# Self-attention in straight code on all engines, and one on-chip sum done by an accumulating transfer instead of GpSimd

## The chip, the cores and the metric

One core of a Trainium2 chip runs the whole program. Its engines work side by side and meet at semaphores: TensorE (PE) multiplies, and loads its weights (PEld) beside that; VectorE (DVE) and ScalarE (ACT) compute and read the matmuls' results; GpSimd (POOL) computes and issues transfers; SyncE (SP) only issues transfers. 16 DMA engines move the data. The metric is the device time of one execution in microseconds (us), median of the runs of a kernel.

## What is computed

A transformer block on x (2 x 2048 tokens, 512 features): self-attention with 16 heads of 32, attention to a short context, and an MLP, each with a layer norm ahead and a residual behind it. The change is in the self-attention, so this is the part that matters (cut):

```python
xn = layer_norm(x, ln0_w, ln0_b)
qkv = xn @ qkv_w.T
q, k, v = jnp.split(qkv, 3, axis=-1)
q, k, v = (_heads(q), _heads(k), _heads(v))       # B, 16 heads, 2048, 32
attn = jnp.einsum('bhnd,bhmd->bhnm', q, k) * SCALE
attn = jax.nn.softmax(attn, axis=-1)
sa = _merge(jnp.einsum('bhnm,bhmd->bhnd', attn, v)) @ sa_proj_w.T
x = x + sa
...
```

Everything is float32. The softmax of one query runs over all 2,048 keys of its batch.

## The kernel before

The phases follow each other: `token_phase` (norm and q, k, v), `self_phase` (the attention itself, functions from L1253 on), a small context phase, cross attention, another `token_phase`, and the MLP. Only `self_phase` is changed.

**Tiling.** The 128 features of four heads are a group. A stage is 512 queries of one group; there are 2 batches x 4 groups x 4 = 32 stages. A stage runs over 2,048 keys in 16 tiles of 128 keys, for four heads: 64 pieces of scores [128 keys x 512 queries].

**Two passes.** The first pass computes the scores to find each query's maximum (64 matmuls into `first`, L1538; VectorE reduces each, L1707). The maxima are turned once per stage by a matmul against the identity (`turn_max`, L1560), split and put beside the queries as extra rows. The second pass (64 matmuls into `second`, L1568) computes the scores less the maximum; ScalarE takes the exponential into `expo` (L1657), which holds 8 tiles of keys. `weigh` (L1581) multiplies them by the values into `weighted`, 128 of the matmuls that the profile counts.

**The order on TensorE** is written out by hand. A stage has eight blocks. In a block, eight matmuls of the second pass of this stage alternate with eight of the first pass of a later one; behind them come those of `weigh` for the two tiles of the block before. Behind block 1 stands `add_up` for the stage before: the sums of its exponentials.

**The sums of the exponentials** are the denominators, one per head and query. GpSimd adds the exponentials of two neighbouring tiles of keys, all four heads at once: `add_pair` (L1474 to L1478), eight pairs a stage, 128 x 2048 elements. A pair's tiles can be overwritten by ScalarE when it is summed. The pair sums go to four parts of the buffer `part_sum`. Pairs 0 and 1 make h0 and h1, and pairs 2 to 5 are added to these in turn by a transfer that accumulates in place: `add_half` (L1480 to L1484), issued by GpSimd when the pair's sum is done; pairs 2 and 4 go from part p0 to h0, pairs 3 and 5 from p1 to h1. Its landing is told by the semaphores `half_added[0]` and `half_added[1]`, 16 each time. Pair 6 is summed to p0 and added to h1 by GpSimd itself (L1514, the merge). Pair 7 is summed to p1. In the next stage the parts change roles: the new h0 is the old p0 and the new p0 the old h0, while h1 and p1 stay.

`add_up` (L1585) then lets ones-matmuls sum over the keys of a part, in three sets: h0, h1 (with pair 6 in it) and p1 (pair 7). The total is copied by ScalarE (L1674), spread by SyncE, inverted by VectorE (L1724), spread again, and GpSimd multiplies the stage's result by it (`divide`, L1489).

**What sets the order around the change.** Each engine runs its own list in order; an instruction that waits holds all behind it on its engine. GpSimd's list per stage is: pairs 0, 1, 2, transfer, pair 3, transfer, `divide` of the stage before, pair 4, transfer, pair 5, transfer, pair 6, merge, pair 7. `pair_done` counts nine per stage (`n_adds`).

**Loops.** TensorE, ScalarE and SyncE have stage 0 written out, then a loop of 3 rounds of 8 stages, then 7 stages written out. VectorE's loop repeats every stage (29 times), GpSimd's every two stages (15 times). In loops a semaphore's target is computed with register instructions. Before a DMA, a wait against a register stands alone with an increment of its own (`wait_alone`); a wait against a number stands by itself.

## Time and profile before

| | |
|---|---|
| median of 3 runs | 3608.2 us (3604.48 to 3614.65) |
| the profiled execution | 3612.71 us, of which the span in the profile is 3610.9 us |
| mean TensorE clock granted in it | 0.939 of full speed |
| self-attention, first to last matmul of its kind | some 323 to 2049 us of the span |

| engine | busy in the span | share |
|---|---|---|
| PE | 3297.7 us | 91% |
| PEld | 2149.8 us | 60% |
| DVE | 2085.2 us | 58% |
| POOL | 1743.7 us | 48% |
| ACT | 1544.2 us | 43% |

Times in rows are in microseconds from the span's start. A row of a timeline has the start, the duration, the engine, the line of the code, the operation, what it writes and reads with shapes, how many instructions were put together, and in brackets the idle time of the engine just before, with what ended it. `issue` there means that the engine waited for nothing that the profile shows. `self_second` is the buffer `second`, in which the totals and the turned maxima have a place too. Matmuls overlap, so a matmul's duration is longer than the distance to the next one.

### The profile page before, as it was taken

What the parts mean: (1) busy time and instruction counts of PE and PEld (TensorE: products, weight loads), DVE (VectorE), ACT (ScalarE), POOL (GpSimd) and SP (SyncE); (2) the same over time, 40 slices, a digit from 0 to 9 for tenths busy, and PEclk for the clock granted to TensorE, in tenths of its full rate; (3) what the DMA queues carried; (4) which work ended last, traced back from release to release, by engine and by line L of the source; (5) the groups of instructions that cost most, each with busy time, mean ns of one, the idle gap of its engine ahead of it and who ended that gap; (6) DMA issues with size and microseconds to landing.
All of it is one profiled execution on the core that took longest, in us unless ns stands there. A gap on an engine that the chain in (4) does not pass through costs nothing. (4 is left out here: it accounts for less than half of the span.)

```text
span 3610.9 us, 52559 instructions
## 1 busy us (share of the span) xinstructions
PE 3297.7 (91%) x16448; PEld 2149.8 (60%) x16448; DVE 2085.2 (58%) x3635; ACT 1544.2 (43%) x2826; POOL 1743.7 (48%) x539
## 2 busy tenths in 40 slices
PE   7998999999999999999999668898968599999999
PEld 5885555555555555555555156566526488888887
DVE  4445877777877777787776025767646542222222
ACT  3230566666666566666666312444423221111111
POOL 0001798888898888889889622343332100000000
PEclk9997999999999999999999778999958799999999
DMA  4447358465664746566455343344325731111110
GB/s 171 180 163 194 78 108 168 103 141 113 127 135 101 165 99 143 114 126 136 99 121 106 89 141 105 122 118 126 93 98 198 263 113 47 47 47 46 47 47 24
DMA packets 195911, 420.97 MB, mean 117 GB/s; under 512 B 33602, under 2 KB 56712, under 8 KB 176240
## 3 DMA queue, kind: packets, MB, share of 16 engines
q1 hardware_dynamic: 173167, 282.80, 25.8%
q0 software_dynamic: 18432, 134.23, 19.1%
q8 instruction: 137, 2.24, 0.3%
q10 hardware_dynamic: 4096, 1.06, 0.1%
q14 instruction: 79, 0.64, 0.1%
HBM read 154.47 MB, written 102.82 MB: 71 GB/s over the span
## 5 line engine op out<-in xcount | busy, mean ns | idle before, releaser
L1707 DVE TENSOR_REDUCE self_part_max<-self_first 128x1 f32<-128x512 f32 x2048 | 1253.0, 679 | 372.5 <-PE self_first L1538 371.9
L1657 ACT ACTIVATE self_expo<-self_second 128x512 f32<-128x512 f32 x2048 | 1042.4, 625 | 504.2 <-PE self_second L1568 500.8
L1477 POOL TENSOR_TENSOR self_part_sum<-self_expo 128x2048 f32<-128x2048 f32 x256 | 1194.3, 4675 | 99.5 <-ACT self_expo L1657 59.9
L1538 PE MATMUL self_first<-self_k,self_q 96*128 96x512 f32 x2048 | 863.5, 429 | 26.4 <-DMA self_k<-k_t 12.8
L1568 PE MATMUL self_second<-self_q,self_k 98*128 98x512 f32 x2048 | 832.5, 408 | 14.7 <-DVE self_max_low L1719 9.8
L1538 PEld LDWEIGHTS self_first<-self_k,self_q 96*128 96x128 f32 x2048 | 401.8, 196 | 330.7 <-DVE self_part_max L1707 173.8
L1581 PE MATMUL self_weighted<-self_expo,self_v_sb 128*32 128x512 f32 x4096 | 498.1, 605 | 0.0
L1568 PEld LDWEIGHTS self_second<-self_q,self_k 98*128 98x128 f32 x2048 | 393.7, 193 | 161.5 <-ACT self_expo L1657 49.6
L2047 DVE CAST mlp_h_high<-mlp_h 128x512 fp32r<-128x512 f32 x128 | 54.8, 428 | 508.1 <-PE mlp_out_sum L61 507.0
L2022 ACT ACTIVATE mlp_h<-mlp_hidden_sum,mlp_b_col 128x512 f32<-128x512 f32 x128 | 88.1, 688 | 603.7 <-PE mlp_hidden_sum L61 603.6
L1581 PEld LDWEIGHTS self_weighted<-self_expo,self_v_sb 128*32 128x32 f32 x4096 | 107.6, 109 | 241.2 <-ACT self_expo L1657 134.3
L989 ACT ACTIVATE cross_expo<-cross_second 77x512 f32<-77x512 f32 x256 | 144.7, 591 | 217.6 <-PE cross_second L840 213.6
L738 POOL TENSOR_TENSOR cross_pair_sum<-cross_expo 77x2048 f32<-77x2048 f32 x32 | 146.2, 4567 | 182.0 <-ACT cross_expo L989 182.0
L59 PE MATMUL mlp_hidden_sum<-mlp_xt_high,mlp_w_high 128*128 128x512 f32 x512 | 203.8, 398 | 24.4 <-DMA mlp_xt_low<-xn_t 24.4
L60 PE MATMUL mlp_hidden_sum<-mlp_xt_low,mlp_w_high 128*128 128x512 f32 x512 | 203.2, 397 | 0.0
L60 PE MATMUL mlp_out_sum<-mlp_w_low,mlp_h_high 128*128 128x512 f32 x512 | 202.4, 395 | 0.0
L61 PE MATMUL mlp_hidden_sum<-mlp_xt_high,mlp_w_low 128*128 128x512 f32 x512 | 202.3, 395 | 0.0
L61 PE MATMUL mlp_out_sum<-mlp_w_high,mlp_h_low 128*128 128x512 f32 x512 | 202.2, 395 | 0.0
L59 PE MATMUL mlp_out_sum<-mlp_w_high,mlp_h_high 128*128 128x512 f32 x512 | 201.9, 394 | 0.0
L1514 POOL TENSOR_TENSOR self_part_sum<-self_part_sum 128x2048 f32<-128x2048 f32 x32 | 146.7, 4584 | 71.8 <-DMA self_part_sum<-self_part_sum 71.8
L1112 DVE TENSOR_REDUCE cross_row_max<-cross_first 128x2 f32<-128x308 f32 x256 | 113.6, 455 | 90.9 <-PE cross_first L823 90.9
L1482 POOL DMA_DIRECT2D self_part_sum<-self_part_sum x128 | 111.8, 873 | 74.9 <-POOL self_part_sum L1477 60.4
(163 smaller groups left out, 4019.3 us busy)
## 6 DMA issues: line engine op xcount, KB each, us to landing
self_part_sum<-self_part_sum POOLq DMA_DIRECT2D x128, 1024.0 KB, 7.5
self_k<-k_t SPq DMA_DIRECT2D x96, 256.0 KB, 10.3
self_q<-q_t SPq DMA_DIRECT2D x93, 256.0 KB, 8.1
cross_q<-cross_r_high SPq DMA_DIRECT2D x256, 64.0 KB, 2.0
qkv_x<-in_x SPq DMA_DIRECT2D x8, 1024.0 KB, 5.3
v<-qkv_v_sb SPq DMA_DIRECT2D x32, 256.0 KB, 2.0
q_t<-qkv_r_high SPq DMA_DIRECT2D x32, 256.0 KB, 2.0
q_t<-qkv_r_low SPq DMA_DIRECT2D x32, 256.0 KB, 2.3
```

The lines of the kernel that those rows point to most:

```text
L59: nc.tensor.matmul(out, left_high, right_high, start=first, stop=False)
L60: nc.tensor.matmul(out, left_high, right_low, start=False, stop=False)
L61: return nc.tensor.matmul(out, left_low, right_high, start=False, stop=last)
L738: nc.gpsimd.tensor_tensor(pair_sum[0:width, g % pair_slots], expo[0:width, u], expo[0:width, u + 1], ALU.add).then_inc(pair_done, 1)
L989: nc.scalar.activation(expo[0:width, unit % e_slots, a], second[0:width, at % s_ring], ACT.Exp, scale=scale).then_inc(exp_done, 1)
L1477: nc.gpsimd.tensor_tensor(to, expo[:, t % p_slots], expo[:, (t + 1) % p_slots], ALU.add).then_inc(pair_done, 1)
L1514: nc.gpsimd.tensor_tensor(part_sum[:, h1], part_sum[:, h1], part_sum[:, p0], ALU.add).then_inc(pair_done, 1)
L1538: nc.tensor.matmul(first[:, n % f_ring], q[0:base, c % q_slots, a, s * P:(s + 1) * P], k[0:base, c // stages_per_group % 2, a, k0:k0 + TOK ...
L1568: nc.tensor.matmul(second[:, s_slot[n]], k[0:exp_rows, c // stages_per_group % 2, a, t * P:(t + 1) * P], q[0:exp_rows, c % q_slots, a], st ...
L1581: mm = nc.tensor.matmul(weighted[cols], v_sb[:, t, cols], expo[:, t % p_slots, a], start=t == 0, stop=t == n_k - 1)
L1657: nc.scalar.activation(expo[:, t % p_slots, a], second[:, s_slot[n]], ACT.Exp, scale=scale).then_inc(exp_done, 1)
L1707: nc.vector.tensor_reduce(part_max[:, a * SUB + s, k:k + 1], first[:, n % f_ring], AX_X, ALU.max).then_inc(first_read, 1)
```

## The change

On every engine the loops of the self-attention become loops of the generator: all 32 stages are written out, and every wait is against a number. GpSimd's merge of pair 6 (L1514) is gone. Instead pair 6 is added to h0 by a fifth accumulating transfer, issued behind its sum, so `half_added[0]` counts 48 a stage, and `pair_done` counts eight. `add_up` takes the parts in another order, h1, then pair 7 (p1), then h0. Pair 0 of a stage waits for the landing of the fifth transfer of the stage before, since it writes to the part that this reads; pair 1 waits for the first set of ones-matmuls instead of the first two, and pair 2, which writes over the old h0, for all three.

```diff
-    n_adds = n_pairs + 1
...
-                with sp.Fori(0, rounds - 1) as r:
+                for r in range(rounds - 1):
...
                 def add_half(i, p, u, half, part):
-                    ge(pool, pair_done, n_adds * i + p + 1, alone=True)
+                    ge(pool, pair_done, n_pairs * i + p + 1, alone=True)
...
                 def add_pairs(i, c):
                     h0, h1, p0, p1 = sum_parts(c)
-                    ge(pool, pair_done, n_adds * i)
+                    ge(pool, half_added[0], 48 * i)
                     add_pair(i, 0, part_sum[:, h0])
-                    ge(pool, total_done, n_sums * (i - 1) + 2)
+                    ge(pool, total_done, n_sums * (i - 1) + 1)
                     add_pair(i, 1, part_sum[:, h1])
+                    ge(pool, total_done, n_sums * i)
                     add_pair(i, 2, part_sum[:, p0])
                     add_half(i, 2, 0, h0, p0)
-                    ge(pool, total_done, n_sums * i)
                     add_pair(i, 3, part_sum[:, p1])
...
                     add_pair(i, 6, part_sum[:, p0])
+                    add_half(i, 6, 0, h0, p0)
                     ge(pool, half_added[1], 32 * i + 32)
-                    ge(pool, pair_done, n_adds * i + 7)
-                    nc.gpsimd.tensor_tensor(part_sum[:, h1], part_sum[:, h1], part_sum[:, p0], ALU.add).then_inc(
-                        pair_done, 1)
                     add_pair(i, 7, part_sum[:, p1])
...
-                with pool.Fori(1, stages // 2) as r:
+                for r in range(1, stages // 2):
...
-                    for n, part in enumerate((h0, h1, p1)):
+                    for n, part in enumerate((h1, p1, h0)):
                         if n == 0:
-                            ge(pe, half_added[0], 32 * (i + 1))
+                            ge(pe, half_added[1], 32 * (i + 1))
                         elif n == 1:
-                            ge(pe, pair_done, n_adds * i + n_pairs)
+                            ge(pe, pair_done, n_pairs * (i + 1))
                         else:
-                            ge(pe, pair_done, n_adds * (i + 1))
+                            ge(pe, half_added[0], 48 * (i + 1))
...
-                with pe.Fori(0, rounds - 1) as r:
+                for r in range(rounds - 1):
...
-                with act.Fori(0, rounds - 1) as r:
+                for r in range(rounds - 1):
...
-                with dve.Fori(1, stages - 2) as i:
+                for i in range(1, stages - 2):
```

The semaphores of one phase are used again by the next, so the lists below name them by the first phase's names: `qkv_xt_high_done` is `exp_done`, `qkv_xt_ready` is `pair_done`, `qkv_xt_stored0` and `qkv_xt_stored1` are `half_added[0]` and `[1]`, `qkv_high_done` is `total_done`, `qkv_var_done` is `first_read`.

GpSimd from the sum of pair 5 to the wait ahead of pair 0 of the next stage, in the kernel before (inside its loop; `REGISTER_ALU` and `ISA` rows compute targets, and carry waits):

```order
L1477 TENSOR_TENSOR self_part_sum<-self_expo 128x2048 [waits qkv_xt_high_done]
L52 REGISTER_ALU
L1482 DMA self_part_sum<-self_part_sum 128x2048 [waits qkv_xt_ready]
L1358 REGISTER_ALU
L1358 REGISTER_ALU [waits qkv_xt_stored0]
L1477 TENSOR_TENSOR self_part_sum<-self_expo 128x2048 [waits qkv_xt_high_done]
L1358 REGISTER_ALU [waits qkv_xt_stored1]
L1514 TENSOR_TENSOR self_part_sum<-self_part_sum 128x2048 [waits qkv_xt_ready]
L1358 REGISTER_ALU
L1477 TENSOR_TENSOR self_part_sum<-self_expo 128x2048 [waits qkv_xt_high_done]
L1358 ISA
L1358 ISA [waits qkv_xt_ready]
```

The same place, from pair 5's transfer on, in the changed kernel:

```order
L1481 DMA self_part_sum<-self_part_sum 128x2048 [waits qkv_xt_ready]
L1476 TENSOR_TENSOR self_part_sum<-self_expo 128x2048 [waits qkv_xt_high_done,qkv_xt_stored0]
L1481 DMA self_part_sum<-self_part_sum 128x2048 [waits qkv_xt_ready]
L1476 TENSOR_TENSOR self_part_sum<-self_expo 128x2048 [waits qkv_xt_high_done,qkv_xt_stored1]
L1476 TENSOR_TENSOR self_part_sum<-self_expo 128x2048 [waits qkv_xt_high_done,qkv_xt_stored0]
L1476 TENSOR_TENSOR self_part_sum<-self_expo 128x2048 [waits qkv_xt_high_done,qkv_high_done] x2
```

The merge between pairs 6 and 7 has become a transfer, the register rows are gone, and pair 0 has a wait for that transfer.

TensorE at `add_up`, behind the matmuls of `weigh` in block 1, before:

```order
L1601 MATMUL self_second<-self_part_sum,self_ones 32x512 [waits qkv_xt_stored0,qkv_xt_high_done]
L1601 MATMUL self_second<-self_part_sum,self_ones 32x512 x3
L1358 REGISTER_ALU
L1601 MATMUL self_second<-self_part_sum,self_ones 32x512 [waits qkv_xt_ready]
L1601 MATMUL self_second<-self_part_sum,self_ones 32x512 x3
L1358 REGISTER_ALU
L1601 MATMUL self_second<-self_part_sum,self_ones 32x512 [waits qkv_xt_ready]
L1601 MATMUL self_second<-self_part_sum,self_ones 32x512 x3
```

And in the changed kernel:

```order
L1598 MATMUL self_second<-self_part_sum,self_ones 32x512 [waits qkv_xt_stored1,qkv_xt_high_done]
L1598 MATMUL self_second<-self_part_sum,self_ones 32x512 x3
L1598 MATMUL self_second<-self_part_sum,self_ones 32x512 [waits qkv_xt_ready]
L1598 MATMUL self_second<-self_part_sum,self_ones 32x512 x3
L1598 MATMUL self_second<-self_part_sum,self_ones 32x512 [waits qkv_xt_stored0]
L1598 MATMUL self_second<-self_part_sum,self_ones 32x512 x3
```

The last set now waits for a landing and not for a sum of GpSimd.

## Rows read from the trace of the kernel before

**Rows 1.** Stretches: us, busy of PE, PEld, DVE, ACT, POOL, clock, DMA, GB/s.

```profile
406.85:1970.26 1563.41, 1509.88 (x8431) 833.87 (x8430) 1196.75 (x2040) 1006.32 (x1980) 1373.87 (x419) 0.99 0.58 123
1970.26:2049.21 78.95, 68.22 (x309) 21.23 (x305) 0.81 (x3) 41.83 (x83) 68.55 (x21) 0.87 0.46 97
```

**Rows 2.** Timeline of PE: turning matmuls, one per stage.

```profile
406.85 0.27 PE L1560 MATMUL self_second<-self_identity,self_row_max 128*16 128x128 f32 x1
...
818.53 0.27 PE L1560 MATMUL self_second<-self_identity,self_row_max 128*16 128x128 f32 x1
...
876.13 0.27 PE L1560 MATMUL self_second<-self_identity,self_row_max 128*16 128x128 f32 x1
...
926.10 0.27 PE L1560 MATMUL self_second<-self_identity,self_row_max 128*16 128x128 f32 x1
...
1970.26 0.27 PE L1560 MATMUL self_second<-self_identity,self_row_max 128*16 128x128 f32 x1
```

**Rows 3.** Timeline of PE: the first matmul behind each jump back.

```profile
836.37 0.79 PE L1538 MATMUL self_first<-self_k,self_q 96*128 96x512 f32 x1 [5.82 <-issue]
...
1256.23 0.79 PE L1538 MATMUL self_first<-self_k,self_q 96*128 96x512 f32 x1 [5.06 <-issue]
```

**Rows 4.** Waits, 406.85 to 1970.26: who for whom, total us, times, longest.

```profile
PEld self_second L1601 <- POOL self_part_sum L1477: 47.7, 23, 3.8
```

**Rows 5.** Timeline of PE: the ones-matmuls of one stage.

```profile
1102.15 1.90 PE L1601 MATMUL self_second<-self_part_sum,self_ones 128*32 128x512 f32 x16
1106.15 1.64 PE L1601 MATMUL self_second<-self_part_sum,self_ones 128*32 128x512 f32 x8 [2.11 <-POOL self_part_sum L1477]
```

**Rows 6.** POOL by line, 406.85 to 1970.26: busy us, mean ns, idle before.

```profile
L1477 POOL TENSOR_TENSOR self_part_sum<-self_expo 128x2048 f32<-128x2048 f32 x240 | 1120.0, 4676 | 49.6 <-DMA self_part_sum<-self_part_sum 28.8 <-ACT self_expo L1657 10.8 <-PE self_second L1601 5.2
L1514 POOL TENSOR_TENSOR self_part_sum<-self_part_sum 128x2048 f32<-128x2048 f32 x30 | 137.6, 4588 | 68.2 <-DMA self_part_sum<-self_part_sum 68.2
...
L1489 POOL TENSOR_TENSOR self_mean<-self_inverse,self_mean 128x512 f32<-128x512 f32 x30 | 47.3, 1576 | 1.3 <-DMA self_inverse<-inverse_rows 1.3
```

**Rows 7.** Timeline of POOL: transfers and waiting sums of one stage.

```profile
1068.22 0.87 POOL L1482 DMA_DIRECT2D self_part_sum<-self_part_sum  x1 [0.58 <-POOL self_part_sum L1477]
...
1076.86 4.57 POOL L1477 TENSOR_TENSOR self_part_sum<-self_expo 128x2048 f32<-128x2048 f32 x1 [0.39 <-DMA self_part_sum<-self_part_sum]
1082.02 0.87 POOL L1482 DMA_DIRECT2D self_part_sum<-self_part_sum  x1 [0.59 <-DMA self_part_sum<-self_part_sum]
1082.63 4.88 POOL L1477 TENSOR_TENSOR self_part_sum<-self_expo 128x2048 f32<-128x2048 f32 x1
1088.09 0.88 POOL L1482 DMA_DIRECT2D self_part_sum<-self_part_sum  x1 [0.58 <-POOL self_part_sum L1477]
1089.49 4.58 POOL L1477 TENSOR_TENSOR self_part_sum<-self_expo 128x2048 f32<-128x2048 f32 x1 [0.52 <-DMA self_part_sum<-self_part_sum]
1097.02 4.60 POOL L1514 TENSOR_TENSOR self_part_sum<-self_part_sum 128x2048 f32<-128x2048 f32 x1 [2.94 <-DMA self_part_sum<-self_part_sum]
```

**Rows 8.** Timeline of POOL in stage 1, already written out: a transfer's issue.

```profile
443.18 0.87 POOL L1482 DMA_DIRECT2D self_part_sum<-self_part_sum  x1 [0.30 <-POOL self_part_sum L1477]
```

**Rows 9.** DMA, 406.85 to 1970.26: a queue (packets, MB, share), and transfers (KB, landing us).

```profile
q0 software_dynamic: 17183, 125.17, 41.1%
...
self_part_sum<-self_part_sum POOLq DMA_DIRECT2D x119, 1024.0 KB, 7.6
```

**Rows 10.** Timeline of ACT: end of pair 6's exponentials, and all of pair 7's.

```profile
1080.42 3.05 ACT L1657 ACTIVATE self_expo<-self_second 128x512 f32<-128x512 f32 x6 [0.44 <-PE self_second L1568]
...
1085.29 4.03 ACT L1657 ACTIVATE self_expo<-self_second 128x512 f32<-128x512 f32 x8 [1.82 <-PE self_second L1568]
```

**Rows 11.** Timelines of PEld, ACT and POOL: the end of the phase.

```profile
1997.06 0.16 PEld L1601 LDWEIGHTS self_second<-self_part_sum,self_ones 128*32 128x32 f32 x8 [1.77 <-POOL self_part_sum L1477]
...
2025.68 4.03 ACT L1657 ACTIVATE self_expo<-self_second 128x512 f32<-128x512 f32 x8 [3.10 <-PE self_second L1568]
...
2042.65 4.51 POOL L1477 TENSOR_TENSOR self_part_sum<-self_expo 128x2048 f32<-128x2048 f32 x1
```

More of the change, by code:

```diff
@@ L1503, in add_pairs @@
                         divide(i - 1)
-                    ge(pool, half_added[0], 32 * i + 16)
+                    ge(pool, half_added[0], 48 * i + 16)
                     add_pair(i, 4, part_sum[:, p0])
@@ L1653, in exponential @@
                             p = (t - p_slots) // 2
-                            ge(act, pair_done, n_adds * i + p + 1 if p >= 0 else
-                               n_adds * (i - 1) + p + n_pairs + 1 + (p == -1))
+                            ge(act, pair_done, n_pairs * i + p + 1)
                     ge(act, second_done, n_seconds * i + n + 1)
```

2 lines of the change are left out of this document (1 added, 1 removed).

## The prediction

> **What bounds the kernel now.** The change touches self-attention alone, some 1,690 of 3,611 us, so I read that stretch first. In the table of stretches [rows 1] TensorE is busy 1,509.88 of 1,563.41 us (97%), POOL 1,373.87 (88%), DVE 77%, ACT 64%. TensorE looks like the bound, but a busy share says nothing about which wait ends last, so the next view is the cadence. A stage turns its row maxima once, so the starts of that matmul are a clock of one tick per stage [rows 2]. From 406.85 to 1970.26 there are 30 ticks: 1,563.41 us, 52.11 us a stage. But single stages take 49.97 us (876.13 to 926.10), and 9 of the 30 take 49.97 to 50.06. So 49.97 us is what TensorE's own instructions need; the other 64.3 us (1,563.41 - 30 x 49.97) are stalls, and only these can be won.
>
> Two kinds are seen. (a) Twice TensorE stands for "issue", 5.82 and 5.06 us [rows 3], on the first matmul of a stage. They are the two places where its loop of eight stages jumps back; the loop's entry and its exit show no such gap. The stage with the first takes 57.60 us (818.53 to 876.13), 7.63 over the floor: 5.8 of gap and some slow matmuls behind it. (b) In the list of waits [rows 4] the sum of a stage's exponentials stands out: TensorE's weight loads before the ones-matmul waited 47.7 us for POOL's last pair sum, 23 times. In the stage shown the third set of these matmuls starts at 1106.15 with 2.11 us idle before it, although the first two sets were through at 1104.05 [rows 5].
>
> Why is POOL late? Its work per stage [rows 6]: eight pair sums of 4.68 us on average, the merge at L1514 with 4.59, the product 1.58, and four transfer issues, each 0.58 us idle and 0.61 until the next instruction starts (1082.02 to 1082.63) [rows 7]. That is 37.4 + 4.6 + 1.6 + 4 x 1.19 = 48.3 us, and then it waits for its own transfers: 0.39 + 0.52 + 2.94 us in the stage shown, 68.2 + 28.8 = 97.0 us over the 30 stages [rows 6], 3.2 a stage. 48.3 + 3.2 = 51.5 us, above TensorE's 49.97. So POOL's chain of adds and landings is the real bound of most stages, and TensorE pays at the one place where it needs POOL.
>
> **The change, part by part.**
> *The merge goes, a fifth transfer comes.* POOL loses 4.58 us (L1514) and gains one issue. Pair 7's add, which had to stand behind the merge, now stands right behind that issue.
> *Constants in POOL's waits.* With registers the issue starts 0.58 us after its pair's sum [rows 7]. In the first two stages, which are written out already, it is 0.30 us [rows 8]. So an issue costs 0.30 + 0.61 = 0.91 us. A sum right behind an issue takes 4.88 and not 4.57 (1082.63, 1076.86), and there is one more of these: 0.3. POOL: 37.4 + 0.3 + 5 x 0.91 + 1.6 = 43.9 us a stage, 6 below TensorE's floor.
> *The new landings.* The chain that can still be long is through the buffers: pair sums 0, 1, 2, transfer, pair 4, transfer, pair 6, transfer (the new one), and pair 0 of the next stage writes over the part that this last one reads. That is 5 adds of 4.57, three gaps of 0.3 and three landings d: 23.7 + 3d. From issue to the start of the add that waits for it the rows show 8.64 (1068.22 to 1076.86), 7.47 (1082.02 to 1089.49) and 8.93 (1088.09 to 1097.02) [rows 7]; the median landing over the stretch is 7.6 [rows 9]. 23.7 + 25.0 = 48.7 us, under 49.97 by 1.2. The bound is passed where d averages 8.76.
> *What TensorE waits for.* It now takes h1, then pair 7, then h0 with the new transfer. With POOL no longer behind, pair 7 can start when its exponentials are there, at 1089.32 in the stage shown; pair 6's were there at 1083.47 [rows 10]. Pair 6's sum, 0.3 and 8.9 of landing are 13.8 us, with a wait of 1 to 2 us for the transfer of pair 4 about 15.5: h0 is complete at 1099.0, where TensorE wants it at 1104.05 [rows 5]. Cover of 5 us. New waits on POOL: pair 0 of the next stage waits for that same landing, 1099.0, and is through at 1103.6; pair 1 waits for the first set of ones-matmuls, through at 1103.1, and ends at 1108.2; pair 2's exponentials come at about 1089.3 + 3 x 5.8 + 2.8 = 1109.5 (blocks of 5.8 us as between pairs 6 and 7, the ones-matmuls between). So POOL has caught up by then. Behind the waiting instructions stand only later pairs, which nobody has missed yet. So nearly nothing of (b) is left; I keep 3 us, 0.1 a stage, for landings that meet the query and key loads.
> *No loops.* TensorE's two jumps go: 7.63 + (7.63 - 0.76) = 14.5 us. The other engines' jumps I price at zero: 9 stages keep the floor although DVE jumps in every one of them, and POOL jumps in every second. Constants give TensorE nothing that I can see: 49.97 us is reached with registers in the waits. Straight code has to be fetched too. The stretch shows two stalls for issue in all on TensorE, both at jumps [rows 3], and the straight last seven stages show none: priced at zero, at worst 5.4 us each.
>
> By the Trainium skill (Runtime: NRT & Kernel Launch, Instruction fetch mechanics) a taken jump out of the resident window must fetch first, while sequential code is fetched ahead, mostly hidden. The two gaps agree; for loops that fit in the window it asks for nothing, which the stages at the floor don't contradict. It would change the sum only if its "mostly" failed.
>
> *The end of the phase.* In the last stage nothing hides POOL. Today: pair 7's sum starts at 2042.65 and ends at 2047.16, and the last set follows [rows 11]. Pair 6's exponentials are ready at 2025.68 + 4.03 = 2029.71; 4.6 + 0.3 + 7.9 gives 2042.5, a gain of 4.7. The stage before this also had a stall in its ones-matmuls, at 1997.06, that lies outside my 30 ticks: 1.77 less the 0.30 that stands between such loads anyway, 1.5. Together 6.2 us.
>
> Sum: 14.5 + (64.3 - 14.5 - 3.0) + 6.2 = 67.5 us. Span 3,610.9 - 67.5 = 3,543.4; the profiled execution took 3,612.7, so 3,545.2 for its like. It is 4.5 above the median of the three runs (3,608.2). I take the median: 3,540.7, say 3,541 us.
>
> **The rivals.**
> *Landings bound the stage.* The software queue holds 41.1% of the 16 engines [rows 9]; a fifth transfer makes it about 51%, on top of the loads. If d averages 9.0, stages take 23.7 + 27.0 = 50.7 us: 1.4 x 30 = 42 us won, and 6: 3,560 us. For it: 8.93 for the transfer that meets the query load. Against: a transfer occupies the engines 5.4 us (41.1% of 1,563 over 119) and they are issued 6 us apart. This is where the Trainium skill (DMA: Bandwidth & Descriptors, Issuing engines are not separate DMA queues) speaks against the change: transfers from all engines share the same 16 and interleave, so the fifth is not free. By it alone I would expect this rival.
> *The other side: the landings take the merge's place and more.* Same place, pair 0 and the last set of ones-matmuls waiting for the new transfer, but with d at 9.8: 23.7 + 29.4 = 53.1 us a stage, 1.0 x 30 = 30 us lost (the jumps' time is inside today's 52.11), less 6 at the end: about 3,632 us. It is slower than now from d = 9.55 up (52.3 us a stage). Today's longest waits of this kind are about that; as an average it would need the loads to crowd every one.
> *Straight code stalls.* If TensorE stood 5.4 us at some twelve places in its long straight stream, 65 us would be lost and the time stay at about 3,606. Against it: the last seven stages.
> *It doesn't do what it says:* POOL's merge was never what is waited for. Then only the jumps are won, 3,594 us. The wait at 1106.15, released by POOL's last sum right behind the merge, speaks against it.
>
> **How the numbers follow.** A measurement here can tell about 0.3% (11 us) from no change. Forecast 0.76; landings bound the stage 0.14; only the jumps 0.02; straight code stalls 0.04 (no change); landings much worse 0.04 (slower). So faster 0.92, same 0.04, slower 0.04. Low end: nothing left of the stalls (3 us), the clock of TensorE staying up at the end of the phase (granted 0.87 from 1970 to 2049 [rows 1], half of that stretch's missing 13%: 5 us), and a run at the low end of the spread (4): 3,529. High end: half of the first rival, up to d = 9.05, 3,563. That leaves out less than 2 in 10.
>
> **What would show it.** Right: nearly every stage at 49.97 us; no "issue" gap over 5 us; waits of TensorE for the ones-matmul under 5 us in all; POOL waiting for exponentials where it now waits for landings; transfers issued 0.3 us behind their sums, 160 of them instead of 128; the last set some 5 us sooner behind the last exponentials. Wrong: stages at 50.5 or more with POOL's pair 0 or 6 waiting for landings (first rival), "issue" gaps in mid-stage (third), or matmul spacing other than now.

## The result, and the profile after

The changed kernel takes 3,584.45 us (median of 6 runs, 3,577.38 to 3,592.35), the kernel before 3,608.14 (6 runs beside them, 3,604.48 to 3,614.65). The ratio is 0.9932, with a 95% interval of 0.9918 to 0.9946. It is faster by 24 us; 67 were forecast, and the time lies above the range (3,529 to 3,563).

The stretches come first, with the same columns as [rows 1]: the 30 ticks; one stage that begins a new group of heads; the stage behind it; the last part of the phase.

```profile
407.47:1948.87 1541.40, 1505.38 (x8431) 825.50 (x8429) 1194.45 (x2040) 1003.70 (x1980) 1268.28 (x419) 0.99 0.69 145
970.43:1027.19 56.76, 52.95 (x283) 28.16 (x282) 39.88 (x68) 33.64 (x66) 44.29 (x16) 0.94 0.85 189
1027.19:1077.20 50.01, 49.67 (x282) 27.48 (x281) 39.80 (x68) 33.42 (x66) 41.19 (x15) 1.00 0.61 130
1009.00:1016.00 7.00, 6.51 (x23) 2.61 (x24) 3.63 (x7) 1.19 (x2) 5.96 (x3) 0.54 0.55 116
```

The 30 ticks fell from 1,563.41 us [rows 1] to 1,541.40, so 22.0 us were won there. From the last tick to the end of the last ones-matmul it was 78.95 us before [rows 1]; now it is 2020.31 - 1948.87 = 71.44 (the row of the last set stands below), so 7.5 were won. Together that is the 29.3 us by which the profiled span is shorter (3,610.9 to 3,581.6), but for 0.2. (The runs' medians differ by 24: the profiled execution of the kernel before, 3,612.7 us, stands 4.6 above its median, the one of the changed kernel, 3,583.4, stands 1.1 below.)

The floor of 30 x 49.97 = 1,499.1 us is missed by 42.3. Where these are is seen from the ticks. 24 of the 30 stages take 49.64 to 50.27 us, 1.1 us over the floor in all. The other six are the stages 4, 8, 12, 16, 20 and 24, each the first of a new group of heads: 57.02, 55.72, 56.76, 57.56, 55.90 and 58.11 us, in all 341.07, which is 41.2 us over the floor. So the whole loss sits in every fourth stage. Ticks around stage 12, from the timeline of PE:

```profile
970.43 0.28 PE L1557 MATMUL self_second<-self_identity,self_row_max 128*16 128x128 f32 x1
...
1027.19 0.28 PE L1557 MATMUL self_second<-self_identity,self_row_max 128*16 128x128 f32 x1
...
1077.20 0.28 PE L1557 MATMUL self_second<-self_identity,self_row_max 128*16 128x128 f32 x1
```

What is different in the first stage of a group? There SyncE issues, beside the three loads of queries of every stage, the twelve loads of the next group's keys (256 KB each, 3 MB). The timeline of SyncE in stage 12:

```profile
980.57 2.27 SPq L1365 DMA_DIRECT2D self_q<-q_t  x3
982.87 8.82 SPq L1365 DMA_DIRECT2D self_k<-k_t  x12
...
999.04 2.42 SPq L1404 DMA_DIRECT2D self_sums<-self_inverse  x4
```

And the timeline of POOL for the same time. The transfer at 982.46 is the fifth, for pair 6 of the stage before; the sum at 985.60 is pair 7's, and the one at 997.31 is pair 0's, which must wait for the fifth to land:

```profile
982.46 0.86 POOL L1481 DMA_DIRECT2D self_part_sum<-self_part_sum  x1 [0.30 <-POOL self_part_sum L1476]
985.60 4.59 POOL L1476 TENSOR_TENSOR self_part_sum<-self_expo 128x2048 f32<-128x2048 f32 x1 [2.28 <-DMA self_part_sum<-self_part_sum]
997.31 13.63 POOL L1476 TENSOR_TENSOR self_part_sum<-self_expo 128x2048 f32<-128x2048 f32 x3 [7.12 <-DMA self_part_sum<-self_part_sum]
...
1046.82 4.59 POOL L1476 TENSOR_TENSOR self_part_sum<-self_expo 128x2048 f32<-128x2048 f32 x1 [2.47 <-ACT self_expo L1653]
```

The fifth transfer is issued 0.41 us ahead of the keys and lands at about 997.3, after 14.8 us. In the six stages it lands after 14.8 to 16.8 us, in the other 24 after 7.6 to 11.5, 9.5 in the median. The DMA engines are busy 85% of this stage, and 61% of the next. In the next stage POOL waits for exponentials (1046.82), as forecast. What the late landing does to TensorE and VectorE is seen in their rows (the first is a weight load; the third and fourth are of VectorE and of TensorE's first pass):

```profile
997.29 0.16 PEld L1598 LDWEIGHTS self_second<-self_part_sum,self_ones 128*32 128x32 f32 x8 [2.06 <-DMA self_part_sum<-self_part_sum]
...
1002.23 1.92 PE L1578 MATMUL self_weighted<-self_expo,self_v_sb 128*32 128x512 f32 x16
...
1008.64 0.25 DVE L1720 RECIPROCAL self_sums<-self_sums 128x16 f32<-128x16 f32 x1 [2.73 <-DMA self_sums<-self_inverse]
...
1009.49 0.79 PE L1535 MATMUL self_first<-self_k,self_q 96*128 96x512 f32 x1 [2.32 <-DVE self_part_max L1703]
...
1011.50 3.64 PE L1578 MATMUL self_weighted<-self_expo,self_v_sb 128*32 128x512 f32 x16
```

The story has three steps. TensorE's last set of ones-matmuls waits for the landing (weights at 997.29). With it the totals are late, and the four small transfers that spread them are issued (999.04) while key loads are still out: the last of the twelve lands at 1007.31, the four small ones right behind it, from 1007.45 to 1008.62. The first takes 8.4 us, where the median is 1.7. VectorE waits for them with its reciprocal (1008.64, 2.73 us), and its row maxima stand behind that; TensorE's first pass waits for a maximum (1009.49, 2.32 us). The granted clock falls in this gap, at 1008.7, and stays at the lower of its two levels (1.2 GHz) for 6.8 us; from 1009 to 1016 it is 0.54 on average, and 16 matmuls of `weigh` take 3.64 us instead of 1.92. The list of waits, 407.47 to 1948.87, gives the sums over all stages (us, times, longest):

```profile
POOL self_part_sum L1476 <- DMA self_part_sum<-self_part_sum: 180.6, 80, 11.3
PEld self_second L1598 <- DMA self_part_sum<-self_part_sum: 18.9, 6, 7.1
DVE self_sums L1720 <- DMA self_sums<-self_inverse: 14.2, 5, 3.3
PE self_second L1598 <- DMA self_part_sum<-self_part_sum: 13.5, 6, 6.2
PE self_first L1535 <- DVE self_part_max L1703: 12.1, 5, 2.9
PEld self_second L1598 <- POOL self_part_sum L1476: 0.6, 2, 0.3
```

Six waits, five waits: these are the six stages. Stage 24 differs from the other five: 6.2 of the 13.5 us stand in it, on one longer wait for the landing, and behind it neither the reciprocal nor a first-pass matmul waits. 13.5 + 12.1 = 25.6 us of TensorE's idle time are named here. Most of the other 15.6 of the 41.2 is the clock: TensorE is busy 1,505.38 us in the 30 ticks, and 1,492.48 in a kernel without these gaps (`e5_no_key_burst`, below), 12.9 more for the same matmuls. The granted clock is at its lower level once in each of the six stages, for 30.6 us together, and nowhere else in the 30 ticks; in `e5_no_key_burst` it never is.

What [rows 4] showed, 47.7 us for POOL's last sum, is 0.6 now. The DMA answers of the same stretch (first from the view of the tile `part_sum`, then from the issues: KB, median us to landing) name the cause in numbers:

```profile
DMA to landing us min/median/max: 6.9/7.8/16.8
...
self_part_sum<-self_part_sum POOLq DMA_DIRECT2D x149, 1024.0 KB, 7.8
self_k<-k_t SPq DMA_DIRECT2D x72, 256.0 KB, 14.5
```

The median of all moved from 7.6 [rows 9] to 7.8 only. The longest moved from 9.6 to 16.8. And the end of the phase, from the timeline of PE, with the last set of ones-matmuls:

```profile
2017.14 1.07 PE L1598 MATMUL self_second<-self_part_sum,self_ones 128*32 128x512 f32 x8 [2.43 <-POOL self_part_sum L1476]
2018.66 1.65 PE L1598 MATMUL self_second<-self_part_sum,self_ones 128*32 128x512 f32 x8 [0.46 <-DMA self_part_sum<-self_part_sum]
```

### The profile page after: what moved, and what is told of

Its sections match the earlier page's. It is cut to its first block and busy times, and to the rows that moved or that the text cites. A ratio compares the mean times of both kernels' runs of the same rounds, so it can differ in the third digit from the quotient of the medians.

```text
span 3581.6 us, 44623 instructions
## 1 busy us (share of the span) xinstructions
PE 3285.9 (92%) x16448; PEld 2138.4 (60%) x16448; DVE 2083.3 (58%) x3635; ACT 1542.4 (43%) x2826; POOL 1628.4 (45%) x539
## 5 line engine op out<-in xcount | busy, mean ns | idle before, releaser
L1481 POOL DMA_DIRECT2D self_part_sum<-self_part_sum x160 | 139.9, 874 | 50.5 <-POOL self_part_sum L1476 44.4
L823 PEld LDWEIGHTS cross_first<-cross_k,cross_q 98*128 98x128 f32 x512 | 109.0, 227 | 51.1 <-DVE cross_row_max L1112 25.6
```

The source lines that it names most:

```text
L1481: pool.dma_start(part_sum[:, half].rearrange("p a t -> p (a t)"), part_sum[:, part].rearrange("p a t -> p (a t)"), accum_op=ALU.add).then_inc(
```

## The experiments

Two theories stood against each other at first. **Burst:** the twelve key loads of a new group meet the fifth transfer, and what is lost is the six stages. **Landings in general:** five transfers a stage load the DMA engines so much that some land late whatever else runs. A third question came with them: which part of the change won what. All diffs are from the changed kernel, but where it is said. The kernel before took 3,608.5, 3,610.4 and 3,609.2 us beside the three sets of runs. "Excess" is the time of the 30 ticks less 1,499.1 us.

### The key loads one head at the start of each stage

```diff
-                    if qt == 0 and not last_group:
-                        for a in range(heads):
-                            load_k(g + 1, (c // stages_per_group + 1) % 2, a)
+                    if not last_group:
+                        load_k(g + 1, (c // stages_per_group + 1) % 2, qt)
```

> The changed kernel, but the next group's keys are loaded head by head, one head at the start of each of the four stages of a group, instead of all four heads (12 transfers) at the start of the first. Theory (crowding): in the changed kernel six stages, every fourth, take 55.7 to 58.1 us and all others 50.0, because the fifth transfer is issued just before the burst of keys and lands 15 to 17 us later. Spread out, all 30 stages take 50.0 to 50.5 us: some 38 us less than the changed kernel, about 3546 us. Rival (the fifth transfer is late at a change of group for another reason, or the straight code stalls there): the six stages stay at 56 us, time as the changed kernel's 3584 us.

Measured: 3,627.3 us, 1.0054 of before (1.0034 to 1.0073), slower than both kernels. The expectation was wrong, and in an instructive way. From the list of waits, 407 to 1948:

```profile
PEld self_second L1597 <- DMA self_part_sum<-self_part_sum: 72.4, 27, 5.0
```

27 waits instead of 6; the fifth transfer lands after 13.2 us in the median. Of the first 27 stages 22 take over 50.5 us, and 12 of these 54.4 to 57.8. The loads had been moved to the very place in each stage where the fifth transfer is out, so every stage has six loads there instead of every fourth having fifteen. Three more 256 KB loads beside the transfer are enough to make TensorE wait. It speaks for the theory that the place matters, and against my picture of a cover of 5 us that only a big burst could eat.

### The burst at the end of SyncE's list of that stage

The burst as it is, but issued last in the stage, behind the store of the results.

```diff
-                    if qt == 0 and not last_group:
-                        for a in range(heads):
-                            load_k(g + 1, (c // stages_per_group + 1) % 2, a)
...
                     v_free(2)
+                    if qt == 0 and not last_group:
+                        for a in range(heads):
+                            load_k(g + 1, (c // stages_per_group + 1) % 2, a)
```

> The changed kernel, with the burst of 12 key transfers whole, but moved to the end of SyncE's list for the first stage of a group, behind the spreading of the sums and the store of the stage before. Crowding theory: the burst then meets neither the fifth transfer of the stage before nor the small transfers of the sums; it meets the transfers of pairs 2 to 5, which have some slack: six stages at 50.0 to 52 us, 3546 to 3556 us. If the burst costs its bandwidth wherever it stands: six stages stay at 55 us or more, 3580 us.

Measured: 3,612.1 us, 1.0006 (0.9994 to 1.0019): no gain over before, and 28 us worse than the changed kernel. Again six stages are slow, but each one tick later (5, 9, 13, 17, 21, 25; 57.5 to 62.5 us, in a profiled execution of 3,598.7 us, the fastest of the ten). The trouble moved with the burst, which is what the burst theory says. Timelines of SyncE and POOL:

```profile
1024.36 8.63 SPq L1365 DMA_DIRECT2D self_k<-k_t  x12
```

```profile
1028.77 0.88 POOL L1481 DMA_DIRECT2D self_part_sum<-self_part_sum  x1 [0.30 <-POOL self_part_sum L1476]
...
1045.26 4.57 POOL L1476 TENSOR_TENSOR self_part_sum<-self_expo 128x2048 f32<-128x2048 f32 x1 [9.82 <-DMA self_part_sum<-self_part_sum]
```

Here the burst met the transfers of pairs 4 and 5: pair 6's sum at 1045.26 had to wait 9.82 us for the one issued at 1028.77, which was out for 16.4. The longest landing of an accumulating transfer in this run is 19.0 us, the longest in all runs. The small transfer of `max_low` was late too: in the stage shown it landed after 11.5 us, where its median is 3.6, and TensorE waited 11.8 us for it in 6 waits. ScalarE issues that one, and not SyncE. So other transfers beside the burst land late too, not the fifth alone, and not only those that GpSimd issues.

### No key loads after the first group's

The keys of the groups 1 to 7 are not loaded, and every group is computed with the first group's keys; the rest is as in the changed kernel.

```diff
-                    if qt == 0 and not last_group:
-                        for a in range(heads):
-                            load_k(g + 1, (c // stages_per_group + 1) % 2, a)
...
-                            ge(pe, k_loaded[a], 48 * (2 * r + c // stages_per_group + 1))
+                            ge(pe, k_loaded[a], 48)
```

> The changed kernel without the loads of the keys of groups 1 to 7: the first group's keys serve all groups, so the scores of the others are of the wrong keys and that work is left out; all other work is the same. If the twelve key transfers at the start of a group are what makes six stages slow: all 30 stages at 50.0 to 50.1 us and the fifth transfer landing in 8 to 10 us everywhere, 3544 to 3548 us. If the sixth stages are slow for another reason (the load of values there, the straight code): they stay at 56 us, 3584 us.

Measured: 3,553.3 us, 0.9839 (0.982 to 0.9859). The stretch of the 30 ticks, columns as above, and the longest landing:

```profile
408.32:1911.44 1503.12, 1492.48 (x8430) 823.88 (x8428) 1193.76 (x2040) 1002.71 (x1980) 1269.18 (x419) 1.00 0.65 136
```

```profile
DMA to landing us min/median/max: 6.9/7.8/11.6
```

Every stage takes 49.78 to 50.33 us, the clock is 1.00, and no weight load of the ones-matmuls waits for a transfer. The excess is 4.0 us instead of 42.3, so the key loads are behind all but some 4 us of it. Five transfers a stage run here as in the changed kernel, so the second theory falls. But the fifth is slower than the others here too: in the six stages it lands after 8.8 to 11.6 us without any key load. TensorE just doesn't feel it. Of the 14.8 to 16.8 us in the changed kernel the key loads account for 3.1 to 4.5 in five of the stages and for 8.0 in stage 24. The time is 5 us above the top of what was expected: a stage takes 50.10 us and not 49.97, 4 us in all. What makes that tenth of a microsecond I did not trace.

### Only the straight code, with the merge kept

This is the kernel before with its five loops written out and nothing else:

```diff
-                with pool.Fori(1, stages // 2) as r:
+                for r in range(1, stages // 2):
```

and the same for `sp`, `pe`, `act` and `dve`.

> The kernel before with its self-attention written out on all engines, and nothing else (the merge on GpSimd stays, nine counts a stage). By my sum: the two jumps of TensorE give 14.5 us, and GpSimd saves 0.28 us at each of four transfers and 0.17 at two sums, 1.4 us a stage, which its 51.5 us chain passes on: 15 to 40 us less than before, 3570 to 3593 us, with waits of TensorE for GpSimd's last sum left. Rival (constants give nothing): 14 us less, 3594 us. Rival (the straight code has a cost of its own that the fifth transfer hid): 3608 us or more.

Measured: 3,561.3 us, 0.9877 (0.985 to 0.9905): better than the changed kernel by 23 us. One row of the stretches and two of the waits:

```profile
407.87:1924.54 1516.67, 1494.01 (x8431) 821.05 (x8430) 1194.08 (x2040) 1003.52 (x1980) 1374.35 (x419) 1.00 0.60 126
```

```profile
POOL self_part_sum L1514 <- DMA self_part_sum<-self_part_sum: 60.0, 30, 4.2
PEld self_second L1601 <- POOL self_part_sum L1477: 21.2, 18, 3.5
```

The merge at L1514 is there, and yet the excess is 17.6 us. The 47.7 us of waits for POOL's last sum [rows 4] are 21.2 here. The six stages take 51.4 to 52.9 us with the same burst of key loads in them, and the longest landing is 9.7 us. Stage 12 shows why, first POOL, then SyncE:

```profile
968.35 0.88 POOL L1482 DMA_DIRECT2D self_part_sum<-self_part_sum  x1 [0.30 <-POOL self_part_sum L1477]
```

```profile
974.38 7.35 SPq L1366 DMA_DIRECT2D self_k<-k_t  x12
```

The last transfer of the stage, pair 5's, is issued 6.0 us ahead of the keys and lands after 9.2 us, so two thirds of its time are over when they come. The fifth is issued 0.4 us ahead of them. The lead alone doesn't explain the difference, though: in the stages 16 and 20 of this run pair 5's transfer has only 1.9 and 1.5 us of it and still lands after 9.6 and 9.2. Why so little is enough stays open.

### Only the fifth transfer, in loops

The changed kernel with its five loops put back.

```diff
-                for i in range(1, stages - 2):
+                with dve.Fori(1, stages - 2) as i:
```

and the same for the other four engines.

> The fifth transfer instead of the merge, but with all loops kept. Crowding theory: six slow stages of 56 to 58 us as in the changed kernel, the others 50.0 except the two at TensorE's jumps (7 us each): 3584 + 14 = 3598 us, GpSimd's register work being hidden. Rival (the crowding comes from the straight code, such as its instruction fetches): no stage above 51 us but the two at jumps, 3560 us.

Measured: 3,615.5 us, 1.0016 (1.0003 to 1.003). By its own the transfer in the merge's place costs a little instead of winning. The waits of TensorE:

```profile
PEld self_second L1598 <- DMA self_part_sum<-self_part_sum: 52.2, 13, 9.0
...
PE self_first L1535 <- issue: 10.1, 2, 5.4
```

The six stages take 56.7 to 60.9 us (58.2 us over the floor in all), 17 us more than in straight code, and the two jumps 57.98 and 57.59 (in a profiled execution of 3,623.5 us, 8 above the median). The expectation was 17 us too low, since it took over the six stages as they are in straight code. With its issue gap still at 0.58 us POOL issues the fifth transfer later (14.2 to 17.0 us behind the tick in the six stages, against 11.2 to 15.1), and the waits are longer.

### Only GpSimd's loop written out

From the kernel before; all other engines keep their loops.

```diff
-                with pool.Fori(1, stages // 2) as r:
+                for r in range(1, stages // 2):
```

> The kernel before with GpSimd's list alone written out with constants; all other engines keep their loops, the merge stays. Straight code with the merge on all engines gave 3561 us, 47 below before. If GpSimd's register instructions are what the other 33 us came from: 3561 + 14.5 for TensorE's two jumps = 3576 us, stages at 50.0 but for the jumps and the six with the burst. If the constants of the other engines mattered: 3590 us or more.

Measured: 3,562.0 us, 0.9868 (0.985 to 0.9887), 14 us better than expected and level with straight code everywhere. TensorE's jumps are still there: their stages take 57.50 and 55.89 us, 13.4 over the floor. Without these the excess is 18.0 - 13.4 = 4.6 us. The waits:

```profile
PE self_first L1538 <- issue: 8.9, 2, 4.6
...
PEld self_second L1601 <- POOL self_part_sum L1477: 0.6, 2, 0.3
```

So GpSimd's written-out list took (b) of the prediction away by itself, 47.7 us of waits to 0.6, with the merge in place. It has constants in its waits and no jumps any more, and no run parts the two. The traces point to the constants: before the transfers' issues POOL is idle for 38.3 us here and for 70.5 in the kernel before, while between its sums, where the jumps are, it stood idle for 4.5 us in all there, never over 0.2. It also shows that `e3_straight_only` could be better: there the six stages lose 12.7 us, here 3.8, with the same instructions on GpSimd. In stage 8 the transfer of pair 5 is issued 7.65 us behind the tick in `e3_straight_only` and 6.03 behind it here. What holds POOL back there stays open.

### The merge kept in one stage of four

If the burst theory holds, it is enough to have no fifth transfer out when the key loads come. Pair 6 of the last stage of each group is merged by GpSimd as before, and in the other stages goes by transfer.

```diff
+    def fifth(i):
+        return i % stages_per_group != stages_per_group - 1
...
                     add_pair(i, 6, part_sum[:, p0])
-                    add_half(i, 6, 0, h0, p0)
+                    if fifth(i):
+                        add_half(i, 6, 0, h0, p0)
                     ge(pool, half_added[1], 32 * i + 32)
+                    if not fifth(i):
+                        ge(pool, pair_done, adds[i] + 7)
+                        nc.gpsimd.tensor_tensor(part_sum[:, h1], part_sum[:, h1], part_sum[:, p0], ALU.add).then_inc(
+                            pair_done, 1)
```

The counts in the other waits, and the order of the sets of ones-matmuls, follow `fifth`.

> The changed kernel, but in the last stage of each group (the one whose fifth transfer would meet the burst of keys) the merge on GpSimd is back; the fifth transfer stays in the three others. If the transfer hurts only where it meets the burst: the six slow stages fall from 56.9 to 50.5 to 52 us and the others stay at 50.0: 3550 to 3558 us, not above straight code with the merge everywhere (3561 us). If the fifth transfer also pushes the others' landings: some stages above 50.5 beside the six, 3560 us or more.

Measured: 3,556.0 us, 0.9845 (0.9826 to 0.9864). Stage 12 and the 30 ticks:

```profile
959.47:1009.82 50.35, 50.00 (x282) 27.38 (x281) 39.89 (x68) 33.51 (x66) 45.75 (x14) 1.00 0.85 185
407.93:1911.76 1503.83, 1492.24 (x8430) 824.07 (x8429) 1194.33 (x2040) 1003.31 (x1980) 1293.90 (x419) 1.00 0.68 144
```

The stage has the same 85% of DMA as in the changed kernel and takes 50.35 us instead of 56.76. The longest landing is 11.0. DMA engines that are busy for 85% of a stage cost nothing where nobody waits for what they move.

### The key loads a few at a time, in mid-stage

The other way to part them: the twelve loads go out in portions of one or two (one part of a head each) behind the blocks 3, 4.5 and 6 of the first three stages of a group, away from the fifth transfer.

```diff
+                        ge(sp, second_done, n_seconds * i + (24, 36, 48)[spot], alone=True)
+                        for a in ((0, 1), (2,), (3,))[qt]:
+                            load_key_part(g + 1, slot, a, spot)
```

> The changed kernel, with each head's three key transfers taken apart and issued one or two at a time behind blocks 3, 4.5 and 6 of the first three stages of a group, never at a stage's start. One such transfer takes the engines about 1 us and an accumulating one 5.4, so each is late by 1 to 2 us at most. If the crowding needs the loads to come together with the fifth transfer: stages 50.0 to 51, 3546 to 3560 us. If it is only a question of how many bytes move per stage: about the 41 us of excess are spread over 24 stages and the time stays within 3575 to 3590 us.

Measured: 3,555.0 us, 0.9849 (0.983 to 0.9868), the same as the last within the intervals. All the bytes are loaded, all 160 transfers run, and the excess is 9.7 us:

```profile
DMA to landing us min/median/max: 6.9/8.2/12.9
```

```profile
PEld self_second L1613 <- DMA self_part_sum<-self_part_sum: 12.5, 16, 1.8
```

The median landing is longer than in the changed kernel (8.2 against 7.8) and the time is 29 us less: the median says little, the longest much.

### SyncE waits for the fifth landing before the burst

This takes the first step of the story apart from the second: the transfer can't meet the keys, but the small transfers stand behind them all the more.

```diff
                     if qt == 0 and not last_group:
+                        ge(sp, half_added[0], 48 * i)
                         for a in range(heads):
```

> The changed kernel with one wait more: SyncE issues the burst of keys only when the fifth transfer of the stage before has landed. This takes apart the two costs of the burst. The fifth transfer then lands in 9 us or less everywhere and TensorE's ones-matmuls wait under 1 us in all (2 to 7 us in each of six stages in the changed kernel). The small transfers of the sums stand behind twelve key transfers in SyncE's queue, later than now: VectorE's reciprocal should wait 5 us or more in each of the six stages (2.6 to 3.3 in the changed kernel), and TensorE behind it. Time within 3575 to 3600 us: one cost gone, the other grown. If the small transfers don't suffer from the burst itself but only from the late total: the reciprocal waits under 1 us and the time falls to 3550 us.

Measured: 3,602.0 us, 0.9979 (0.9968 to 0.999), slightly above the top of what was expected. The waits:

```profile
DVE self_sums L1721 <- DMA self_sums<-self_inverse: 41.9, 6, 8.2
...
PE self_first L1536 <- DVE self_part_max L1704: 39.5, 6, 7.8
```

There is no wait of the ones-matmuls for a transfer any more, and yet the six stages take 58.1 to 60.0 us: the reciprocal waits 7 us in each, and TensorE with it. The small transfers land after up to 11.1 us. So the second step is a cause in its own right: small transfers issued right behind twelve loads. One part of the expectation missed: the fifth transfer, kept apart from the keys, was to land in 9 us or less everywhere, and takes 8.5 to 12.1 in the six stages.

### The reciprocal four maxima later

```diff
-invert_at, max_sent_after = (3, 1), 55
+invert_at, max_sent_after = (3, 5), 55
```

> The changed kernel with VectorE's reciprocal of the sums four reductions (some 2.5 us) later in its list. If the reciprocal that waits at the head of VectorE's list costs what the slow stages show (2.2 to 2.9 us of TensorE's idle time and 3 us at half clock behind it): the six slow stages fall from 56.9 to about 52 to 53 us, where the wait for the fifth transfer is left: 3584 - 6 x 4.5 = 3557 us. If it is hidden by something else that is late: no change, 3584 us.

Measured: 3,609.1 us, 0.9998 (0.9984 to 1.0012); a miss. The reciprocal no longer waits, as meant. But the waits show what it moved:

```profile
PEld self_second L1598 <- DMA self_part_sum<-self_part_sum: 45.5, 16, 7.0
POOL self_mean L1488 <- DMA self_inverse<-inverse_rows: 37.3, 17, 7.8
```

The product (`divide`) stands in GpSimd's list ahead of pair 4 and needs the inverse. It now waits up to 7.8 us, the transfers of pairs 4 to 6 go out later, and the last set of ones-matmuls waits longer for the fifth. I had looked at who stood behind the reciprocal, and not at who stood behind its consumer.

### Straight code with the gentle key loads, and both remedies at once

`e11_straight_gentle` is `e3_straight_only` with the loads of `e8_keys_gentle`; `e12_hybrid_gentle` is `e6_hybrid` with them.

> No fifth transfer: straight code with the merge on GpSimd, and the key transfers issued one or two at a time in mid-stage as in e8. Straight code alone took 3561 us with 17.6 us over the floor in 30 stages, 10 of them in the six with the burst. If the burst causes these too: about 3549 us. If GpSimd, with 4 us more of work per stage than with the fifth transfer, falls behind because the key transfers now meet pairs 2 to 5: 3560 us or more.

> The fifth transfer in three of four stages, the merge in the last of each group, and the key transfers of e8. The hybrid alone took 3556 us with the six stages at 50.3 to 51.0; e8 alone 3555 with six at 51.1 to 51.4. Together I expect 3551 to 3554 us: only the 50.0 to 50.1 us of the stages and nothing to win beyond. Slower than 3556 would mean that the loads are now spread to where they meet transfers without slack.

Measured: 3,604.7 us, 0.9987 (0.9976 to 0.9999), and 3,562.4 us, 0.9874 (0.9857 to 0.989). Neither wins by it. In the first, the waits are

```profile
POOL self_part_sum L1529 <- DMA self_part_sum<-self_part_sum: 52.0, 29, 4.9
PEld self_second L1616 <- POOL self_part_sum L1492: 50.7, 25, 4.3
```

and the list of [rows 4] is back: with the merge POOL has no time to spare, and loads in mid-stage lengthen the landings that it waits for there. Whether a placement of the loads is good depends on which transfers are waited for at that place.

### The parts side by side

| | merge | fifth transfer | fifth, and merge before the burst |
|---|---|---|---|
| loops | 3,608 to 3,610 | 3,615.5 | |
| straight code | 3,561.3 | 3,584.5 | 3,556.0 |

The straight code wins 31 to 47 us, the transfer loses 7 to 23 as it was built, and wins some 5 where it is kept away from the key loads (the intervals of `e3_straight_only` and `e6_hybrid` overlap slightly, so this 5 is likely and not sure). The versions `e6_hybrid` and `e8_keys_gentle` beat both kernels: 28 to 30 us below the changed one.

## Why the prediction was wrong

**The step that failed** is the last sentence of the part on what TensorE waits for: 3 us kept, 0.1 a stage, for landings that meet the query and key loads. That term measured 42.3 us, 41.2 of them in six stages. Behind it was the cover of 5 us for h0, reckoned with a landing of 8.9. With 42.3 in the place of the 3.0 the sum gives 28.2 us, and 29.5 with the 7.5 of the phase's end, against the 29.3 by which the profiled span is shorter. The 8.9 came from [rows 7], the transfer of pair 5 in a stage in which it meets only the loads of queries. Behind pair 6 the landing is longer even without keys: 9.5 in the median of the 24 stages, and 8.5 to 12.1 in the six where the keys are held back (`e9_keys_behind_fifth`). The 5 us of cover were enough for that. In the first stage of a group it meets twelve key loads as well, and took 14.8 us in the stage shown, more than the 8.9 and the cover of 5 together. The trace of before could not show this landing: its longest was 9.6, and in its six stages the last transfer, pair 5's, was issued 2.5 to 5.5 us ahead of the keys and landed after 8.7 to 9.4. But it did show twelve loads at that place, in one stage of four, and the new transfer's time of issue was worked out in the prediction. The two were not laid over each other; the loads were given a tenth of a microsecond a stage. The ticks of before also marked the place, had I listed them singly and not only counted those at the floor. Its stages 4, 8, 12, 16, 20 and 24 take 53.30, 52.93, 52.30, 56.33, 53.52 and 52.60 us, 53.50 on average against 51.77 for the other 24. Stage 12 of before, from its timeline of PE:

```profile
976.07 0.27 PE L1560 MATMUL self_second<-self_identity,self_row_max 128*16 128x128 f32 x1
...
1028.37 0.27 PE L1560 MATMUL self_second<-self_identity,self_row_max 128*16 128x128 f32 x1
```

The tail of it was not thought of at all: late totals, small transfers that SyncE issues behind the loads, VectorE's maxima behind the reciprocal, and the lower clock behind the gap. In the six stages the waits of the ones-matmuls are 13.5 of the 41.2 us, and 12.1 are the waits behind the reciprocal; most of the rest is the clock.

**The rivals.** The nearest was "landings bound the stage", which put the loss at the right place (pair 0 and the last set waiting for the new transfer) with the wrong distribution: it took an average landing of 9.0 and 0.7 us in every stage. The median hardly moved (7.8), and 24 stages are at the floor. The rule of the Trainium skill (DMA: Bandwidth & Descriptors, Issuing engines are not separate DMA queues) that transfers from all engines share the same 16 and interleave agrees with the late landings, but TensorE paid for them only where the other transfers come in a burst.

**The part that did the work** was misjudged too. The prediction put POOL at 51.5 us a stage, 1.5 over the floor, and had both prices: 4 x 0.28 = 1.1 us for the constants, and 4.6 us for the merge less 0.9 for the issue. It never asked whether the smaller one was enough (by its own figures, 51.5 less 1.1, POOL would still have stood 0.4 above the floor). `e7_pool_straight` shows that it was: with GpSimd's list alone written out only 0.6 us of waits for POOL's last sum are left. POOL waited less for its landings too, 73.4 us against 97.0. The 6 us of slack that the fifth transfer brought were worth some 5 us of time in all, and only where it was kept away from the keys; as built it put a landing on TensorE's path.

**Right, point by point.**
- No jumps: no "issue" gap over 5 us on TensorE; `e4_fifth_in_loops` and `e7_pool_straight`, which keep TensorE's loop, show both again (57.98 and 57.59, 57.50 and 55.89 us), so 13.4 to 15.6 us for the 14.5 forecast.
- Straight code does not stall: rival three fell, since 24 stages take 49.64 to 50.27 us. Most take 50.01 to 50.04; that is 1.1 us over the floor in all 24.
- The issue of a transfer 0.30 us behind its sum, 160 of them. From the groups of the page:

```profile
L1481 POOL DMA_DIRECT2D self_part_sum<-self_part_sum x160 | 139.9, 874 | 50.5 <-POOL self_part_sum L1476 44.4
```

- POOL's work: 1,268.28 us busy in the 30 ticks against 1,373.87, and waits for exponentials in the normal stages.
- "It doesn't do what it says" fell for TensorE's wait: 47.7 to 0.6 us. But half of it was true: the merge was not needed for that.
- The end of the phase: 7.5 us won for the 6.2 forecast.
- "Waits of TensorE for the ones-matmul under 5 us in all" was the test that failed: 18.9 us on the weight loads for the landing, in 6 waits.

## What to carry to other kernels

When a step is moved from an engine to a transfer, find the stage in which the most other loads are out at the moment of its issue, and price the landing there; a median over all stages and all transfers hides it, and who waits for it decides what it costs. List the stages' times singly before and after: a loss in every fourth stage names its cause by itself. And where a change has two parts that press on the same bound, ask which of them alone gets below it.

## What the hardware showed that I had not expected

- An accumulating transfer of 1 MB within the chip's on-chip memory lands after 6.9 us at best and 7.6 to 7.8 in the median. The fifth of a stage, issued just when the twelve loads of 256 KB go out, takes 14.8 to 16.8 us; at the same place without them (`e5_no_key_burst`) it takes 8.8 to 11.6. The longest is 19.0 (`e2_k_late`). Even three loads more at its side make TensorE wait (`e1_k_spread`). By the Trainium skill (DMA: Bandwidth & Descriptors, Queues, rings and completion order) each DMA engine takes work in turns from the queues that have some, a packet at a time. The longer landings agree with such sharing; the turns themselves no run here shows.
- A transfer of 2 KB lands after 1.7 us in the median, but after up to 8.8 us in the changed kernel when its engine has issued twelve loads shortly before, and after up to 11.1 right behind them (`e9_keys_behind_fifth`). One of 8 KB that another engine issues is late beside them as well (11.5 us, `e2_k_late`).
- Gaps of 2.2 to 2.9 us on TensorE, each some 12 us behind one of 1.2 to 1.9, brought the granted clock to its lower level in five stages. The clock cost 12.9 us in the 30 ticks, half as much as the gaps themselves (25.6). The length of a gap alone doesn't tell: two of 2.45 and 2.61 us in `e3_straight_only` were followed by no fall.
- The loop of one engine, GpSimd, with register instructions in its waits, was worth some 48 us of 3,610 (`e7_pool_straight`), though each issue of a transfer lost only 0.28 us by them: they held POOL just above the bound. Writing out the other engines as well brought nothing more beyond the jumps; in the six stages it even cost 9 us, and why stays open.
